# A convolution block with graph attention on one core: convolution groups laid across each other, and one operand of two stages held in PSUM

## The reference

```python
def conv_ref(x):                      # on the normalised input
    A = x
    A, _ = scan(step1: A[..., 32*i:32*i+32] = conv1x1(A, w1) + b1, i in 0..3)
    A = relu(A)
    A, _ = scan(step2: A[..., 32*i:32*i+32] = conv3x3(A, w2) + b2, i in 0..3)
    A = relu(A)
    A, _ = scan(step3: A[..., i] = conv1x1(A, w3) + b3, i in 0..127)
    return A + x

x = x + conv_ref(ln(x, 1e-6))
t = tokens(x)
n = ln(t, 1e-5)                       # input of everything below
h = (n @ W_gat) as [M, 4 heads, 4 experts]
src, dst = edge_index (524288 edges), and a loop for every token
e = leaky_relu(a_src[src] + a_dst[dst], 0.2)
alpha = softmax of e over the edges with the same dst
agg = segment_sum(h[src] * alpha, dst) + b_gat
scores = mean over heads of (layernorm(agg) * gamma + beta)
w = softmax of the two highest of 4 scores, 0 for the others
out = sum over experts: w * (gelu(n @ W1 + b1) @ W2 + b2)
t = t + n + out                       # n: the block's own residual
```

## Time and profile before

| | us |
|---|---|
| median of 3 runs (lowest to highest) | 2852.92 (2850.57 to 2858.71) |
| the profiled execution's own time | 2850.96 |
| its span in the trace | 2848.9 |
| busy: PE / PE weight loads | 1380.4 / 753.7 |
| busy: DVE | 1939.1 |
| busy: ACT | 675.9 |
| busy: POOL | 1417.8 |

### The profile page before, as it was taken

The page is one execution under the profiler, slowest core; times in us unless marked ns, Lnnn a source line. Parts: engine busy times, 40 slices in busy tenths (PEclk is TensorE's granted clock), DMA queues, the critical chain, the costliest instruction groups (busy, mean ns, idle before and its releaser), DMA issues. The chain is left out here.

```text
span 2848.9 us, 19310 instructions
## 1 busy us (share of the span) xinstructions
PE 1380.4 (48%) x6406; PEld 753.7 (26%) x6406; DVE 1939.1 (68%) x2972; ACT 675.9 (24%) x1125; POOL 1417.8 (50%) x1282
## 2 busy tenths in 40 slices
PE   2757578388387799950002370000074555455640
PEld 0225126125323555520001240000042332233320
DVE  4992884795686509999998724940137648765877
ACT  3412442431441333310001120000032313232320
POOL 1000000000000178878778777877677777777772
PEclk9965685595586599975556675555586776777765
DMA  9803101301301422220111214151243454345534
GB/s 359 338 0 36 30 1 30 35 1 30 35 16 30 51 73 77 72 47 12 14 14 44 70 46 40 18 36 15 27 126 111 160 170 153 89 157 172 156 93 124
DMA packets 192961, 221.38 MB, mean 78 GB/s; under 512 B 82202, under 2 KB 167838, under 8 KB 179294
## 3 DMA queue, kind: packets, MB, share of 16 engines
q1 hardware_dynamic: 104094, 119.66, 14.3%
q0 software_dynamic: 45888, 52.77, 10.3%
q10 hardware_dynamic: 42880, 47.73, 5.6%
HBM read 107.01 MB, written 106.76 MB: 75 GB/s over the span
## 5 line engine op out<-in xcount | busy, mean ns | idle before, releaser
L478 POOL DMA_INDIRECT KC<-node_dram,KB x1024 | 1142.1, 1115 | 439.7 <-issue 317.7
L680 PE MATMUL hidden_out<-XT,W 128*128 128x512 f32 x512 | 277.4, 682 | 658.3 <-ACT ARENA_A L831 657.5
L335 POOL DMA_DIRECT2D KB<-KA x8 | 4.1, 522 | 800.7 <-DVEq L1070 800.7
L680 PEld LDWEIGHTS hidden_out<-XT,W 128*128 128x128 f32 x512 | 95.8, 215 | 817.7 <-ACT ARENA_A L831 783.5
L688 PEld LDWEIGHTS Z<-W,ARENA_A 128*128 128x128 f32 x2048 | 272.2, 214 | 112.7 <-issue 112.7
L688 PE MATMUL Z<-W,ARENA_A 128*128 128x128 f32 x2048 | 298.2, 306 | 0.0
L831 ACT ACTIVATE ARENA_A<-hidden_out,b1c 128x512 f32<-128x512 f32 x256 | 174.1, 687 | 443.8 <-issue 309.3
L685 PE MATMUL Z<-b2r,ones 1*128 1x512 f32 x256 | 163.4, 721 | 147.7 <-ACT ARENA_D L839 122.8
L1028 DVE TENSOR_TENSOR KC<-KA 128x1024 f32<-128x1024 f32 (+1 forms) x196 | 199.4, 1018 | 4.9
L1029 DVE TENSOR_TENSOR KC<-KA 128x1024 f32<-128x1024 f32 (+1 forms) x196 | 198.5, 1013 | 0.0
L1231 DVE TENSOR_TENSOR KA<-XG,thresholds 128x3072 bf16<-128x3072 f32 x24 | 80.6, 3358 | 157.5 <-DMA XG<-keys_dram,win_i 156.7
(11 more groups left out here) (293 smaller groups left out, 2160.6 us busy)
## 6 DMA issues: line engine op xcount, KB each, us to landing
payload<-XT SPq DMA_DIRECT2D x2, 20480.0 KB
ye_dram<-ARENA_D ACTq DMA_DIRECT2D x32, 1024.0 KB, 4.2
XT<-ye_dram SPq DMA_DIRECT2D x32, 1024.0 KB, 12.2
KC<-node_dram,KB POOLq DMA_INDIRECT x1024
payload<-KC SPq DMA_DIRECT2D x132, 80.0 KB, 1.7
x_dram<-XG SPq DMA_DIRECT2D x4, 2048.0 KB, 8.7
XG<-x_dram SPq DMA_DIRECT2D x32, 256.0 KB, 9.1
out_dram<-XG ACTq DMA_DIRECT2D x32, 256.0 KB, 3.2
```

Source lines behind the costliest of these rows:

```text
L478: pool.indirect_dma_start(row_buf[0][h][:, t, :], None, node_dram, bass.IndirectOffsetOnAxis(ap=KB[:, col:col + 1].bitcast(I32), axis=0)). ...
L680: pe.matmul(PF[m % 2][:, :], W1[:, m // 2, (m % 2) * P:(m % 2) * P + P], XT[:, n * CHUNK:(n + 1) * CHUNK], start=True, stop=True).then_inc ...
```

## The change

It has three parts.

**1. Groups laid across each other.** Every group gets its own place for x: XG, ARENA_D, a part of XT, and halves of KB and KC. SP loads x of groups 1 and 2 at the start, and x of group 3 after the keys are split; the edges come behind the weights instead of ahead of them. PE's and ACT's programs are no longer written group by group: `conv_half` is one half of a stage, and after each half comes a fixed number of chunks of step 3 of the group before (STEP3_FILL) and of normalising for a neighbouring group (NORM_FILL), in the order NORM_ORDER. Two banks (MB) go round among all these products (`next_bank`). Odd groups use a second padded image at the end of XT, which POOL zeroes (late_pads). The scales are kept twice (scale1, scale1x, shift1) or apart (scale2, shift2). The row b3 is one product of 512 columns instead of four of 128. On DVE, sort steps stand between the chunks of a residual (STEPS_AFTER). POOL's first gather no longer waits for a_dst, which has a semaphore of its own (adst_stored), and of a group's results each piece has its own.

**2. Operands in PSUM.** The limits of the counting are copied to MB[1] (limits_p). In the attention, a_dst and run_max lie in the two MB banks, the exponentials (exp_out, written by ACT's Exp) in TA[0], the mask of unused slots in TA[1]. What used PO moves to TA[1].

**3. The last gates.** The last super of four groups (28 to 31) becomes three: [28, 29], [30], [31]. The gate's instructions act on as many nodes as the super has.

```diff
-SUPERS = NODE_GROUPS // RING
+SUPERS = [list(range(n, n + RING)) for n in range(0, NODE_GROUPS - RING, RING)] + [[28, 29], [30], [31]]
-STEPS = [(23, 3), (44, 8), (44, 8), (44, 8)]
+STEP3_FILL = ((0, 0, 0, 0, 0, 0, 0, 0), (2, 4, 2, 0, 0, 0, 0, 0), (2, 4, 2, 0, 0, 0, 0, 0), (2, 2, 2, 2, 0, 0, 0, 0))
+NORM_FILL = ((0, 2, 0, 2, 0, 2, 2, 0), (0, 0, 0, 3, 3, 3, 3, 4), (0, 0, 0, 3, 3, 3, 3, 4), (0, 0, 0, 0, 0, 2, 3, 3))
+NORM_ORDER = tuple((kind, g, c) for kind, g in ((1, 0), (1, 1), (1, 2), (2, 0), (1, 3), (2, 1), (2, 2), (2, 3))
+                   for c in range(CHUNKS))
+STEPS_AFTER = ((0, 2, 1, 1, 1, 2, 1, 0), (0, 4, 1, 1, 1, 4, 1, 0), (0, 4, 0, 4, 0, 4, 0, 0), (0, 1, 1, 1, 1, 1, 1, 0))
...
+        x_parts = [[XG[:, :]], [ARENA_D[:, 0:TILES * C]], [XT_of[2]], [KB[:, LROW:], KC[:, LROW:]]]
...
+        limits_p = MB[1][:, 0:2 * P]
+        a_dst, run_max = (k[:, :].rearrange("p (l g) -> p l g", g=HEADS) for k in MB)
+        exp_out = TA[0][:, 0:NODES * TERMS * HEADS]
+        unused = TA[1][:, 0:NODES * SLOTS].rearrange("p (c k) -> p c k", k=SLOTS)
...
             pool.wait_ge(S["sources_ready"], 1)
-            pool.wait_ge(S["node_stored"], 32 * GROUPS)
+            pool.wait_ge(S["node_stored"], 16 * GROUPS)
...
+            def step3(g, c):
+                pe.wait_ge(S["relu_out"], g * 16 + 12 + c // (CHUNKS // IMGS) + 1)
+                bank = next_bank((3, g, c), S["x1_ready"], g * CHUNKS + c + 1)
+                pe.matmul(bank[:, :].rearrange("p (t c) -> p t c", c=C), ones[0:1, :], bc(b3_row[:, :], 1, [1, TPC, P]),
+                          start=True, stop=False, skip_group_check=True)
+                for t in range(TPC):
...
-            for g in range(GROUPS):
-                norm_step1(g)
-                convolution(g)
-                step3(g)
-                norm_nodes(g)
+            norm_chunks(CHUNKS)
+            last_chunk()
+            for g in range(GROUPS):
+                chunks = iter(range(CHUNKS))
+                for place in range(8):
+                    conv_half(g, place // 2, place % 2)
+                    if place == 0 and g >= 2:
+                        last_chunk()
+                    for c in islice(chunks, STEP3_FILL[g][place]):
+                        step3(g - 1, c)
+                    norm_chunks(NORM_FILL[g][place])
+                if g == 0:
+                    last_chunk()
...
+            for c in range(CHUNKS):
+                step3(GROUPS - 1, c)
+            norm_chunks(CHUNKS)
...
+            token_stats(0)
+            scales1(0)
             small_weights()
+            token_stats(1)
+            keys = make_keys()
+            next(keys)
+            scales1(1)
+            next(keys)
+            token_stats(2)
+            sort_steps(11)
+            scales1(2)
+            residual(0)
+            sort_steps(5)
+            scales2(0)
+            sort_steps(24)
+            token_stats(3)
+            sort_steps(14)
+            scales1(3)
+            residual(1)
+            sort_steps(8)
+            scales2(1)
+            sort_steps(35)
+            residual(2)
+            sort_steps(8)
+            scales2(2)
+            sort_steps(19)
+            residual(3)
+            scales2(3)
+            sort_steps(ROW)
...
-                            limits = shared(thresholds[:, cols])[:, :, j:j + PAIR_J].rearrange("p c j -> p j c")
+                            limits = shared(limits_p[:, cols])[:, :, j:j + PAIR_J].rearrange("p c j -> p j c")
```

More of the change, by code:

```diff
@@ L820, in _ @@
[L820 to L826 removed]
+                        rewrite(g, i)
+                    elif g < 2:
+                        root1(g + 2)
@@ L887, in attention @@
             def attention(n):
                 act.wait_ge(S["e_ready"], n + 1)
-                act.activation(e_buf, e_buf, ACT.Exp).then_inc(S["e_exp"], 1)
+                act.activation(exp_out, e_buf, ACT.Exp).then_inc(S["e_exp"], 1)
             feed_forward(1)
-            for sg in range(SUPERS):
-                for k in range(0, RING, 2):
-                    chunk = next(chunks, None)
-                    if chunk is not None:
+            for sg, groups in enumerate(SUPERS):
+                wide = len(groups) * NODES
+                for n in groups:
+                    chunk = next(chunks, None) if n % 2 == 0 else chunk
+                    if chunk is not None and n % 2 == 0:
@@ L924, in _, with token_stats, variances @@
             dve.wait_ge(S["consts"], 10)
-            def normalise(n, eps):
+            def token_stats(g):
+                dve.wait_ge(x_in[g], 16 * len(x_parts[g]))
+                for t in range(TILES):
+                    last = dve.bn_stats(bn[:, t, :], x_tile(g, t))
+                link(last)
+                variances(mean_var1, std1, 1e-6, "var1_ready")
+            def variances(mean_var, std, eps, ready):
                 for t in range(TILES):
```

551 lines of the change are left out of this document (308 added, 243 removed).

## The result

| | before | after | predicted |
|---|---|---|---|
| median, us | 2852.34 | 2531.31 (2530.06 to 2534.16, 4 runs) | 2543 |
| ratio | | 0.8872, 95% interval 0.8856 to 0.8888 | 0.891 |
| span | 2848.9 | 2530.2 | 2539 |
| POOL's first gather | 987.0 | 759.0 | 776 |
| from there to the end of the last | 1814 | 1716.4 | 1708 |

The kernel became 11% faster, 12 us more than forecast. The three pieces of the span, which the prediction added up, came within 17, 8 and 0 us.

A forecast was written before the change was run, and what follows sets the result against it. POOL never stops once begun, so the span was three pieces: 776 us before its first gather, 1814 - 74 - 32 of POOL, 55 of tail, 2539 us. That gave a forecast time of 2543 us, range 2485 to 2655.

The forecast's parts named there:

- The start: Convolution groups, before POOL's first gather: laying groups across each other moves that gather from 987 to 776 us.
- PE's chain: PE's work before POOL: start 57, convolution 251, other terms, summing to 712 us until the last group's scales are ready.
- rival D: Before POOL: DVE's floor of 732 us is reached, PE never makes DVE wait; 776 - 44, total 2499 us; 12%.
- hand-overs: Fills begin while ACT still rewrites: 2.2 us for each of 27 fills, 60 us; bounds 0 and 4.6 each.
- the fills: PE's chunks between convolution halves: normalising 2.7 us (step 1) or 2.8 (nodes), step 3 4.8; 66, 67, 115 and 38 us.
- The upper bound of 850: Latest POOL start in us, given as following from the bounds of re-entries and hand-overs; the floor was 732.
- Re-entries: Convolution halves following slow work: 1.8 us lost in each of 27, 49 us; bounds 0 and 7.83 each.
- Rival B: Convolution: PE stays at 1.2 GHz in all halves because slow fills lie between; +130, total 2675 us; 8%.
- The PSUM part: Gathers beside DVE's work: one input in PSUM saves 74 us in the two counting passes and 32 in the attention.
- Rival C: Counting and attention: comparisons hold up POOL from PSUM as well, so nothing is gained; +106, total 2650 us; 8%.
- The tail: After the last gather: split gates, with first sums waiting for loads, take 55 us in place of 48; bounds 40 and 60.
- Rival E: Before POOL: ACT's queue serialises the fills, all 72 filled chunks waiting; +590, total 3130 us, slower than before; 1%.

The follow-up runs named there:

- e6: Changed kernel with two sort steps moved ahead of the first residual: POOL's first gather 10.2 us earlier than in the changed kernel; total time could not be read.
- e1: Changed kernel with the counting's limits read from SBUF again: 2599.64 us, ratio 0.9082.
- e3: Kernel before, with only the counting's limits in PSUM: 2790.86 us, ratio 0.9751 to the kernel before.
- e4: Changed kernel with the last four node groups gated together again: 2525.81 us, ratio 0.8831 to the kernel before.
- e10: Changed kernel with last four groups gated together, first part of keys ahead of group 1's statistics, 14 and 2 sort steps about the first residual: 2519.53 us, ratio 0.8808.

## Why the prediction was right, point by point

- **What bounds the kernel.** Right: three pieces, and POOL the bound of the second. (Of POOL's gaps ahead of L478 three and not one are more than the pause, but the other two are 2.8 and 0.3 us.)
- **The start, 776 against 759.0.** The sum went by PE's chain, and this is its step that failed: DVE's queue set the end. e6 shows it (10.2 us less on DVE's waits, 10.2 us earlier), and so do 693.5 busy us of 759. It is rival D's mechanism, and half of its size: DVE was not without waits (10.5 and 2.4 us for PE, 5.6 for the x of group 1), so 759 lies between its 732 and my 776. That 776 came so near is in part luck, for two errors of the sum cancel. From 64.3 to 696 PE is busy for 473.0 us, where my terms for it add up to 251 + 49 + 66 + 67 + 115 + 38 = 586. And PE's waits for DVE, to which I gave no term, are some 100 us: 57.7 directly, ahead of L685, and by way of ACT 28.1 (the root shown above) and 16 of the 22.2 that end at 605.90, in which ACT waited for DVE's scales. Its other waits, some 50 us, and the 7 at the end are near the 60 for hand-overs and the 9. So the last group's scales were ready at 694.5 and not at 712, and the 64.5 us from there to POOL's start are what I had (64). In the sum, the fills were too dear: at my prices the 32 chunks of each kind are 32 x 2.7 + 32 x 2.8 + 153 = 329 us of PE; the rows have 52.4 + 50.4 + 48.0 + 44.8 and 56.4 for step 3's own products (L689), 252. A chunk of step 3, priced at 4.8 us, takes 4.0 even at 0.50, and 2.14 at the full clock, which 11 of the 24 between halves had. I had priced all at the clock of long stretches of slow work. The other way, the convolution began at 64.3 and not at 57: the weights landed at 24.2 (19), the small weights took 9.4 us (6), the rest 30.7 (32). The upper bound of 850 does not follow from the bounds that were to give it: 162 us more for the re-entries and 64 more for the hand-overs make 1002.
- **Re-entries.** 251 + 49 = 300 us were forecast for the 32 halves; the groups of L675 have 73.4 + 71.1 + 69.6 + 68.3 = 282. Rival B (all at 1.2 GHz, 15.7 us per half) falls with the first half of 7.93.
- **The PSUM part, 106 against 98.** The counting gave 68 to 69 (e1, e3) where I had 74: the gathers gained all that they could, 2 x 45, but POOL then waited 26.4 us for windows to be counted where I had 2 x 8 (before: 2.2). The attention: by the rows 36.9 us were lost on L478 before (415.4 - 401 x 0.944), 7.8 on L518 after (411.8 - 428 x 0.944); with the slots some 33, where I took 32. Rival C falls with e1 and e3. The Trainium skill ("SBUF — State Buffer", Who interferes with whom) reports a probe in which tensor_tensor did not stall a DMA; beside the comparison of e1 a gather, which is a DMA that POOL issues, took 3.98 us, and here the measurement decides. Its other rule, that whoever issues first has the shared ports for its whole instruction and the other is blocked, agrees with the ends at 0.82 and 0.81 us behind the comparison. For the reverse order these traces do not show it: a gather that was first did not lengthen a comparison.
- **The tail, 55 against 54.8.** Right in size and in its reason; by the tails of e4 and e10 (48.1) nearly all of the 7 us lost are the early split's.
- **Rival E** did not come: the chunks of step 3 between halves take 2.14 to 4.0 us, and PE's waits for ACT in the piece are 37.5, 42.0 and 28.1 us in all.

The total came out nearer than its first piece: 17 us too much at the start and 8 too little behind it.

## What to carry to other kernels

Work that moves between bursts of a fast engine can find another clock there than in its old place: give it both prices, since here 11 of 24 chunks were at the full clock and 7 at half of it. When two queues come out within some 6% of each other in a sum (732 and 776), say that both are near, and give the waits of the one for the other a term: here 10 us off DVE's waits gave 10, and 67 us more on PE cost 26. A wait removed on one queue pays only up to that queue's next dependence (5.6 us turned into 5.9 more of another wait). A wait for an engine that is itself idle is a wait for what that engine's program has ahead: look there for the releaser. Where an engine's long instructions with both inputs in SBUF stand beside gathers issued by POOL, moving one small input to PSUM gives the gathers' loss back (of 90 us in the counting some 68 stayed, since POOL then waited for DVE elsewhere), and gating the last pieces early costs time if something must be loaded for them first.
